# Shared PSUM slots for rarely reached entries in a graph-aggregation kernel on one Trainium2 core

## The reference

```python
mask = adj != 0
scores = where(mask, -arange(1024), -inf)
vals, idx = top_k(scores, 25);  valid = vals > -inf
feats = where(valid[..., None], x[idx], -inf)          # per batch
agg = feats.max(axis=2)
degree = mask.sum(-1)
agg = where((degree <= 25)[..., None], maximum(agg, 0.0), agg)
out = relu(concatenate([x, agg], -1) @ W + b)          # W is 256 x 128
return layernorm(x + out)                              # no affine part, eps 1e-5
```

## Time and profile before

| | |
|---|---|
| median of three runs | 766.96 us (761.51 to 767.87) |
| the profiled execution, whole | 749.41 us |
| its span, first to last instruction | 747.7 us |
| TensorE busy, mean granted clock | 585.2 us (78%), 0.922 |
| VectorE busy | 633.1 us (85%) |
| ScalarE busy | 483.4 us (65%) |
| GpSimd busy | 258.4 us (35%) |

### The profile page before, as it was taken

How to read it: one execution, slowest core, us unless ns; L and a number is a source line. 1 busy time by engine, 2 the same in 40 slices (tenths; PEclk the granted TensorE clock), 3 DMA queues, 4 the chain that set the end, 5 groups by cost and what they waited for, 6 DMA issues and landing times.

```text
span 747.7 us, 13348 instructions
## 1 busy us (share of the span) xinstructions
PE 585.2 (78%) x3952; PEld 336.8 (45%) x3952; DVE 633.1 (85%) x948; ACT 483.4 (65%) x911; POOL 258.4 (35%) x309
## 2 busy tenths in 40 slices
PE   3768878978877887888779877797887878877873
PEld 2444544644444444454444544454444444444432
DVE  5888999879987789899978788987998868988893
ACT  6735765569756687478935679465975568644654
POOL 3324413544034430455132531335403534044500
PEclk9699998999999899999988999799999989999996
DMA  7511310422024220432123120231302411011102
GB/s 248 198 36 58 116 36 19 142 61 98 1 84 141 76 76 2 133 120 77 47 79 129 57 87 31 74 133 57 111 2 75 149 56 40 2 51 33 37 1 58
DMA packets 32678, 56.68 MB, mean 76 GB/s; under 512 B 4513, under 2 KB 21154, under 8 KB 32546
## 3 DMA queue, kind: packets, MB, share of 16 engines
q1 hardware_dynamic: 26146, 42.08, 16.7%
q0 software_dynamic: 6400, 13.12, 6.3%
HBM read 50.99 MB, written 4.19 MB: 74 GB/s over the span
## 4 chain that ended last, share of the span: by engine, by line
PE 33%; DVE 23%; issue 19%; ACT 9%; DVEq 7%; another core or an unknown queue 4%; DMA 4%; SPq 1%; ACTq 0%
PE pair L946 21%; DVE part L683 9%; DVE hot L677 4%; DMA adj_sb<-in_adj 4%; PE half L946 4%; DVE agg_t L783 3%; DVEq L755 2%; PE p_V L930 2%; DVEq L815 2%; ACT maskT L480 2%; PE misc L1008 2%; DVE g_feat L754 1%; ACT row_work L611 1%; PE misc L1006 1%
## 5 line engine op out<-in xcount | busy, mean ns | idle before, releaser
L946 PE MATMUL pair<-hot,x_part 128*128 128x512 bf16 (+2 forms) x1608 | 388.3, 381 | 63.6 <-DVE part L683 36.5
L683 DVE TENSOR_REDUCE part<-pair 128x128 f32<-128x1024 f32 x256 | 311.1, 1217 | 86.7 <-PE pair L946 74.4
L946 PEld LDWEIGHTS pair<-hot,x_part 128*128 128x128 bf16 x1608 | 146.8, 101 | 228.3 <-issue 64.6
L397 POOL DMA_INDIRECT g_feat<-in_x,g_idx x200 | 191.2, 956 | 123.5 <-issue 94.8
L434 POOL TENSOR_TENSOR y_sb<-relu_sb,x_sb 128x128 f32<-128x128 f32 x64 | 30.3, 473 | 344.0 <-ACT relu_sb L539 342.8
L783 DVE TENSOR_REDUCE agg_t<-part 128x128 f32<-128x1024 f32 (+2 forms) x56 | 113.4, 2025 | 0.2 <-ACT part L546 0.2
L480 ACT ACTIVATE maskT<-p_maskT 128x1024 bf16<-128x1024 bf16 x56 | 57.0, 1018 | 54.1 <-remote 25.1
L677 DVE TENSOR_SCALAR hot<-V 128x1024 bf16<-128x1024 bf16 x224 | 84.2, 388 | 0.0
L471 ACT ACTIVATE mask<-adj_sb 128x1024 bf16<-128x1024 int32 x56 | 59.0, 1053 | 32.2 <-DMA adj_sb<-in_adj 32.0
L546 ACT ACTIVATE part<-half 128x512 f32<-128x512 f32 x56 | 33.4, 597 | 70.3 <-PE half L946 68.5
L528 ACT ACTIVATE hot<-distance,one 128x1024 bf16<-128x1024 bf16 x56 | 64.1, 1145 | 0.1
(11 more groups left out here) (86 smaller groups left out, 635.1 us busy)
## 6 DMA issues: line engine op xcount, KB each, us to landing
adj_sb<-in_adj SPq DMA_DIRECT2D x56, 512.0 KB
g_adj<-in_adj SPq DMA_DIRECT2D x8, 512.0 KB, 4.0
x_sb<-in_x SPq DMA_DIRECT2D x8, 512.0 KB
out<-y_sb SPq DMA_DIRECT2D x7, 512.0 KB
g_feat<-in_x,g_idx POOLq DMA_INDIRECT x200
out<-y_sb SPq DMA_DIRECT2D x1, 448.0 KB
w_sb<-in_W SPq DMA_DIRECT2D x1, 128.0 KB
out<-y_sb SPq DMA_DIRECT2D x1, 64.0 KB
```

Source lines behind the costliest of these rows:

```text
L397: pool.indirect_dma_start(out=g_feat[w][:, k, :], out_offset=None, in_=x_rows, in_offset=bass.IndirectOffsetOnAxis(ap=g_idx[w][:, k:k + 1] ...
L683: dve.tensor_reduce(part[:, par(q, s), BANK + p], pairs[buffer_of(s, p)][:, :, :, :].rearrange("f a k i -> f i (a k)"), AX.X, ALU.max).the ...
L946: last = pe.matmul(dst, x_part[:, q, part_no, kb], one_hot, start=(part_no == 0), stop=(part_no == 2))
```

## The change

1. `SHARED` names, for each kind of tile, three slots that several entries share. An entry is written (kb, r) with r counted from 1, and r is also the count of set columns from which a row reaches it. The members of a shared slot are picked one after the other into the same 128 columns and add up. That is right as long as no row reaches two of them.
2. `groups` replaces `banks`: slots are laid out in groups of up to eight, of nearly equal size, in the two pair buffers, a shared slot at the end of a group. Groups have 8, 8, 8, 7, 7 slots in tile 1; 8, 8, 8, 8 in tiles 2 and 3; 7, 7, 7, 7 in tiles 4 and 5; 7, 7, 6, 6 in tiles 6 and 7. A piece ends at a bank's border, at rank 6, and where a shared slot begins. The bank `half`, its copy on ScalarE and its semaphores are gone.
3. `reduce_pair` reads only the slots in use. `part` is laid out with the slices innermost, so the merge reads 4 or 5 neighbouring values for each output.
4. `count_violations` also compares the counts with `reach_tab` and marks rows that reach two members of a slot; the mark is worth `APART` = 4096 in the level. A tile so marked is picked a second time without sharing (`FULL`, 5 to 7 groups: `apart_level`, `apart_reduce`), and the extra ranks follow.
5. `p_xt` moves to the bank that `half` had (`turn`), so `rank_product` no longer waits for `s_xtc` nor `transpose_x` for the copies of V.
6. Waits on `s_half` become waits on `s_pair` and `s_xused`. `s_xused` now counts `EXTRAS` per stage.

```diff
-def banks(depths): ...
+SHARED = {1: (((0, 11), (2, 5), (3, 6), (5, 5), (6, 5), (7, 4)),
+              ((0, 10), (1, 7), (3, 5), (4, 5), (6, 4)),
+              ((0, 12), (1, 6), (2, 6), (4, 6), (5, 4), (7, 5))),
+          2: (((1, 6), (2, 4), (6, 4)),
+              ((0, 8), (2, 5), (3, 5), (4, 4), (5, 4), (7, 4)),
+              ((0, 9), (1, 5), (3, 4), (4, 5), (5, 5), (6, 5))),
+          4: (((0, 7), (1, 5), (2, 4), (4, 4), (5, 4), (6, 4), (7, 4)),
+              ((3, 4), (5, 3)),
+              ((6, 3), (7, 3))),
+          6: (((0, 7), (2, 4), (3, 4), (5, 3), (6, 4)),
+              ((0, 6), (1, 5), (4, 4), (5, 4), (7, 3)),
+              ((1, 4), (6, 3), (7, 4)))}
+SHARED.update({3: SHARED[2], 5: SHARED[4], 7: SHARED[6]})
+APART = 4096
+REDO = 2 * APART
...
+def groups(depths, shared):
+
+    taken = {member for slot in shared for member in slot}
+    own = [(kb, r) for kb, d in enumerate(depths) for r in range(d) if (kb, r + 1) not in taken]
+    slots = [[entry] for entry in own]
+    mixed = [[(kb, r - 1) for kb, r in slot] for slot in shared]
+    total = len(slots) + len(mixed)
+    count = -(-total // (2 * BANK))
...
-        part = sb("part", [P, 2, BANK + MAX_PAIRS, P], F32)
+        part = sb("part", [P, 2, P, MAX_GROUPS], F32)
...
-        half = psum("half", [P, 4, P], F32)
+        turn = psum("turn", [P, 512], F32)
...
-        p_xt = p_V[:, 0:P]
+        p_xt = turn[:, 0:P]
...
                 if not (isinstance(m, int) and m < 2):
-                    act.wait_ge(s_half, m - 1)
+                    act.wait_ge(s_xused, EXTRAS * (m - 1))
                 nc.scalar.activation(hot[:, par(q, s), 0], V[:, q, s - 1], ACT.Relu, bias=first_bias[:, 0:1],
...
-            def copy_half(i, q, s): ...
...
-                            dve.wait_ge(s_half, m - 1)
+                            dve.wait_ge(s_pair, picked_two_before(i, q, s))
...
-                dve.tensor_reduce(part[:, par(q, s), BANK + p],
-                                  pairs[buffer_of(s, p)][:, :, :, :].rearrange("f a k i -> f i (a k)"),
+                dve.tensor_reduce(part[:, par(q, s), :, p],
+                                  pairs[buffer_of(q, s, p)][:, 0:SLOTS[s][p]].rearrange("f k i -> f i k"),
                                   AX.X, ALU.max).then_inc(s_used, 1)
...
+            def apart_reduce(i, q, s):
+
+                before = EXTRAS * (pos(i, q, s) + 1) - EXTRA - len(FULL[s])
+                over = len(FULL[s]) - COUNT[s]
+                for p in range(len(FULL[s])):
+                    dve.wait_ge(s_xpair, before + p + 1)
+                    dst = part[:, par(q, s), :, p] if p < COUNT[s] else more[:, :, p - COUNT[s]]
+                    dve.tensor_reduce(dst, pairs[buffer_of(q, s, COUNT[s] + p)][:, 0:FULL_SLOTS[s][p]]
+                                      .rearrange("f k i -> f i k"), AX.X, ALU.max).then_inc(s_xused, 1)
...
-                dve.wait_ge(s_halfc, m + 1)
-                dve.tensor_reduce(agg_t[:, par(q, s)], part[:, par(q, s), 0:BANK + PAIRS[s]].rearrange("f k i -> f i k"), AX.X,
+                dve.tensor_reduce(agg_t[:, par(q, s)], part[:, par(q, s), :, 0:COUNT[s]], AX.X,
                                   ALU.max).then_inc(s_agg, 1)
...
+                for j in range(SHARES):
+                    dve.tensor_tensor(reached[:, j], cnt[:, 0], reach_tab[:, j], ALU.is_ge)
                 dve.tensor_reduce(degree[:, :], cnt[:, 0], AX.X, ALU.add)
                 dve.drain()
+                dve.tensor_reduce(sharing[:, :, :], reached[:, :, :, :], AX.X, ALU.add)
+                dve.drain()
+                dve.tensor_scalar(viol[:, 0, :, NT + 1:].rearrange("p t j -> p j t"), sharing[:, :, :], 1.5,
+                                  float(APART), ALU.is_gt, ALU.mult)
...
                     with dve.If(lv > 0):
-                        with dve.If(lv < LEVELS):
+                        with dve.If(lv < REDO):
+                            with dve.If(lv < APART):
+                                dve.sem_inc(s_xused, EXTRAS - EXTRA)
+                            with dve.Else():
+                                dve.sem_inc(s_xused, EXTRAS - EXTRA - len(FULL[s]))
+                                apart_reduce(i, q, s)
                             extra_hots(q, s)
                             extra_reduce(i, q, s)
...
-                pe.wait_ge(s_xtc, m + 1)
                 pe.matmul(p_V[:, :], rank_bf[:, :], maskT[:, par(q, s), h * N // 2:(h + 1) * N // 2],
                           start=True, stop=True).then_inc(s_Vp, 1)
...
+            def pick_pieces(q, s, pieces, dst, signal):
+                u = par(q, s)
+                for k, (kb, r, n, place, first) in enumerate(pieces):
+                    one_hot = hot[:, u, r:r + n, kb] if r < LOW else hot_high[:, u, r - LOW:r - LOW + n, kb]
+                    pick(dst[:, place:place + n], q, kb, one_hot, signal if k == len(pieces) - 1 else None,
+                         first, all(place != piece[3] for piece in pieces[k + 1:]))
```

More of the change, by code:

```diff
@@ L91, in runs @@
         return list(zip(starts, starts[1:] + [NT]))
+    ALIKE = [(a, max(t for t in SHARED if SHARED[t] == SHARED[a])) for a in SHARED
+             if a == min(t for t in SHARED if SHARED[t] == SHARED[a])]
+    REACHES = 1 + sum(len(slot) for a, _ in ALIKE for slot in SHARED[a])
     TABLES = 8 + sum(len(runs(DEPTHS[kind[0]])) for kind in KINDS)
@@ L168, in build @@
         shift = sb("shift", [P, 2, NT], F32)
-        pairs = [psum(f"pair{i}", [P, 2, 4, P], F32) for i in range(2)]
-        half = psum("half", [P, 4, P], F32)
+        pairs = [psum(f"pair{i}", [P, 2 * BANK, P], F32) for i in range(2)]
+        turn = psum("turn", [P, 512], F32)
         p_maskT = psum("p_maskT", [P, N], BF16)
@@ L771, in redo @@
                 dve.wait_ge(s_ft, m + 1)
-                dve.wait_ge(s_halfc, m + 1)
-                for p in range(BANK + PAIRS[s]):
-                    last = dve.tensor_copy(part[:, par(q, s), p], p_xt)
+                for p in range(COUNT[s]):
+                    last = dve.tensor_copy(part[:, par(q, s), :, p], p_xt)
                 last.then_inc(s_xdone, 1)
```

223 lines of the change are left out of this document (120 added, 103 removed).

## The result

| | before | after |
|---|---|---|
| median of 4 runs | 767.41 us (761.51 to 768.3) | 802.13 us (796.61 to 811.78) |
| profiled execution, span | 747.7 us | 797.2 us |
| granted clock of TensorE | 0.922 | 0.933 |

The recorded ratio is 1.0589, with a 95% interval of 1.0503 to 1.0675. Ratios in this document compare only each kernel's fast executions, within 1.5% of its fastest, while medians take all of them, so the two can differ. Here the medians are 4.5% apart, and the eight times behind them don't reproduce 1.0589, so take the loss as 4.5 to 5.9%. Forecast were 732 us and a range of 702 to 772; by either figure the time lies above it.

The account below looks back on a forecast made before the run. VectorE was taken as the pacemaker, with some 10 us a batch lost at handovers. From 749.4 us, minus 70 for shorter stages, plus 36 for second pickings, came 715, or 732 us on the median; range 702 to 772.

Parts of the forecast that it names:

- VectorE's work: Shorter picking reductions and merges, plus the sharing test, take VectorE from 77.3 to 62.7 us a batch.
- 285 more cost 0.8 us a batch: TensorE's picks: a matmul costs its columns plus 2.7 ns, so 576 a batch for 291 add 0.8 us.
- rival 3: Narrow picks on TensorE cost 83 ns, not 56: 69 us more, 801 us, slower; chance 0.07.
- 10 us per batch "lost at handovers": VectorE is the pacemaker, busy 77.3 of 87.6 us a batch; the rest is idling once a stage for one picking.
- forecast length of 78.5: Sum of the seven forecast stage lengths of a batch, 78.5 us for 87.6, so -9.1 us a batch.
- The handover that was to be late next: At stage ends TensorE waits for VectorE's last reduction and s_xused: 1.4 us idle, 2.6 us after stages 1 to 3.
- Stage 6: VectorE sets this stage, 9.9 us of work plus 0.5: 10.4 us for 12.38.
- Second pickings: Three tiles meet in a shared slot and are picked afresh: +36 us together, between 20 and 45.
- Rival 1: Larger saving: 10 us more of the waits behind xt_sb and 8 us from fewer 1.2 GHz stretches, 714 us; chance 0.17.
- Rival 2: TensorE is late more often, each new bubble bringing a 1.2 GHz stretch: 31 us come back, 763 us; chance 0.18.
- Rival 4: Far jumps over the second picking's code cost 2 us in each of 56 stages: +112 us, 844 us; chance 0.05.
- Rival 5: The change doesn't do what it says: no tile meets in a slot (695 us), or many do; chance 0.03.

Follow-up runs that it names:

- series 1: First follow-up series, parts of the change by themselves: layout of part, one-slot picks, both kernels without tile 0's gathers; the kernel before took 701.51 us.
- b_nogather2: Kernel before without the gathers of tile 0's neighbours: 695.07 us, ratio 0.939, where the kernel before took 748.93 us.
- a_nogather2: Changed kernel without tile 0's gathers, second pickings still in it: 703.26 us, ratio 0.950 to the kernel before at 748.93 us.
- series 4: Fourth follow-up series, on where late signals come from: three kernels without gathers, one with wide picks and no second pickings; the kernel before took 748.93 us.
- a_extract: Changed kernel with tile 0's extraction steps of stages 1 to 3 one reduction earlier: 780.84 us, ratio 1.035 to the kernel before.
- series 2: Second follow-up series, on second pickings and handover: changed kernel, without second pickings, with earlier extraction, and the kernel before again; the kernel before took 753.58 us.
- a_nogather: Changed kernel without tile 0's gathers, run where the kernel before took 701.51 us: 704.35 us, ratio 1.005.
- series 3: Third follow-up series, narrow picks where signals are late: changed kernel, the same with wide picks, kernel before with one-slot picks or part's layout; before took 759.72 us.
- a_wide_ns: Changed kernel with wide picks in place of the shared entries and without the three second pickings: 705.79 us, ratio 0.955 to the kernel before.
- a_nosecond: Changed kernel with a threshold of 99.5 in the sharing test, so without the three second pickings: 734.4 us, ratio 0.964 to the kernel before.
- b_narrow2: Kernel before with every picking one slot wide, 852 picking matmuls a batch for 291: 859.75 us, ratio 1.139 to the kernel before.
- b_part: Kernel before with only the layout of part changed, slices innermost: 676.6 us, ratio 0.967 to the kernel before.

## Why the prediction was wrong, step by step

**VectorE's work: right.** Merges of 512 elements at 675 ns (forecast 680), of 640 at 808 (810), reductions of 768, 896 and 1024 elements at 959, 1087 and 1225 ns (949, 1083, 1217), 546.7 us busy in all. The writes of part at a step of 20 bytes cost at most 4 to 10 ns each.

**"285 more cost 0.8 us a batch": the step that failed.** The 56 ns of the earlier trace rows are right, in series 1 for runs of 24 and in after between halts. What is wrong is the conclusion that a narrow matmul beside a weight load costs only its columns whatever the state of the signals; the sum had no term for late signals at all, though "remote" stands in the earlier trace rows. Under late signals each one more costs 21 to 25 ns, through halts and a lower clock, not through a wider spacing. An estimate for after from that price: 2280 more (6445 - 3952 weight loads, less the 213 of second pickings) x 22 ns = 50 us, 6.3 us a batch where 0.8 stood. This brought the time to where rival 3 had it (801), but rival 3 gave another mechanism, 83 ns for each pick at all times, and series 1 refutes that, and the 81 ns quoted beside it, with runs of 24 at 56 ns. That part of the agreement is luck. By the Trainium skill (TensorE: Matmul & The Clock Gate, Architectural detail) TensorE's queue takes 64 instructions; in the stretch shown, 54 lie between the signal's due time and the first halt behind 346.28, which agrees roughly. Elsewhere it doesn't: counted from the pick whose signal is late to the next halt, the same trace has anything from 3 to 75 instructions at 30 places. A full queue would explain why wide picks suffer less, since a place in it then holds up to four times as much work, but no run measured it, and why TensorE halts stays open.

**The 10 us per batch "lost at handovers": misread, the second step that failed.** The forecast took the distances between VectorE's busy time and the length of a stage in the earlier trace rows to be handovers and carried them over. The kernel without gathers shows what they were. The same batch of b_nogather2 and of a_nogather2:

```profile
sum 81.30, PE 69.28 PEld 39.96 DVE 77.09 ACT 60.80 POOL 7.82; mean PE 9.90 PEld 5.71 DVE 11.01 ACT 8.69 POOL 1.12
```

```profile
sum 76.01, PE 67.02 PEld 53.54 DVE 61.04 ACT 57.40 POOL 7.81; mean PE 9.57 PEld 7.65 DVE 8.72 ACT 8.20 POOL 1.12
```

With 77.1 us of work VectorE needs 81.3, so 4 of the 10 us were handovers and the other 6 went with the gathers. And the saving there is 81.3 - 76.0 = 5.3 us in this batch, not 9.1. Over the six batches that have neither a second picking nor the shorter end, the means are 81.4 and 76.7 us: 4.7 us a batch, over 7.7 batches 36 us. The stages with second pickings are 42 us longer in that trace, so the changed kernel should be 6 us slower without gathers; measured, it is 8.2 (series 4) and 11.8 us (series 1).

With gathers the same six batches take 88.8 us in the trace of before and 89.6 in that of after. So the gathers add 7.4 us a batch to the one and 13.0 to the other: the changed kernel's batches are 4.7 us shorter without gathers and 0.8 longer with them. (The traced execution of before is 18 us below its median; by the medians and the 43 us of second pickings they would be 1.0 shorter with them.) So most or all of the saving goes, and this comparison needs no price for a narrow pick. The forecast length of 78.5 is near the 76.7 without gathers.

**The handover that was to be late next: it isn't.** Forecast was that TensorE idles 2.6 us at the entry to stage 4 in every batch. In a_nogather2:

```profile
255.15 0.38 PE L1002 MATMUL p_V<-maskT,rank_bf 128*128 128x512 bf16 x1
255.84 1.31 PE L1018 MATMUL pair<-hot,x_part 128*128 128x512 bf16 x9 [0.31 <-DVEq L940]
```

and on VectorE at the same time:

```profile
255.35 1.23 DVE L726 TENSOR_REDUCE part<-pair 128x128 f32<-128x1024 f32 x1 [1.52 <-PE pair L1018]
256.49 1.22 DVE L784 MAX8 g_val<-g_score 128x8 f32<-128x1024 f32 x1
```

The first picks of stage 4 start at 255.84, while the last reduction of stage 3 is still under way and MAX8 has not begun. The releaser is DVEq, VectorE's sequencer, which had raised s_xused by then, ahead of its engine. I had read the code as if the count were raised behind the work. A picking's own wait is for the reduction two before it. This fits a_extract, which gained nothing. All waits in front of picks 512 wide, the first of every stage among them, come to 36.7 us in a_nogather2, 4.6 a batch; the forecast had 3 x 2.6 + 4 x 1.4 = 13.4. Its 0.5 us for branch and semaphores had no row behind it either.

**Stage 6: 10.4 forecast, 12.5 measured, 12.8 without gathers.** VectorE's work there fell from 11.91 to 10.09 us and the stage kept its length. The forecast took the larger of two bounds, VectorE's work or TensorE's with a handover. Here is VectorE in a_nogather2, from the last reduction of stage 6 to the merge that ends the window:

```profile
283.44 0.96 DVE L726 TENSOR_REDUCE part<-pair 128x128 f32<-128x768 f32 x1 [1.81 <-PE pair L1018]
...
284.56 3.42 DVE L813 TENSOR_TENSOR g_feat<-g_feat 128x1536 f32<-128x1536 f32 x3 [0.17 <-issue]
...
289.21 1.08 DVE L726 TENSOR_REDUCE part<-pair 128x128 f32<-128x896 f32 x1
```

The window begins at 277.40. TensorE needs until 283.4 for the picks, products and linear layer of stage 6, and VectorE waits for it; then come, one behind the other on VectorE, a reduction, gathered_max from 284.56 to 289.2 and the next stage's first reduction, while TensorE in turn waits 2.5 us, as in the earlier trace rows. TensorE's part and VectorE's part lie in series, 6.0 + 6.8 us, and neither got shorter: the reductions and merge that did lie beside TensorE's part.

**Second pickings: right in kind, 7 to 16 us low.** 45 to 52 us by series 2, 43 by the lengths of stages, for 36. The three stages that hold them are 15.8 (stage 3), 15.8 (stage 6) and 11.1 us (start of the first batch) longer than their like, for 14.1, 12.7 and 9.3. The extra one-hots stand behind the fresh reductions and both engines take turns in it.

**Rival 1** (a larger saving, 714): no. Its clock came, its time didn't: in the seven windows summed above TensorE has its full clock throughout in a_nogather2, where b_nogather2 has 0.86 and 0.89 in the last two. **Rival 2** (TensorE late more often, half clock, 763) named the right place, a loss in the stages TensorE sets, but it priced a lost clock, and the mean clock rose from 0.922 to 0.933. **Rival 4** (far jumps): no; at the forward jump into stage 4 shown above TensorE waited 0.31 us in all, all its picks of a_nogather2 and of a_nogather waited for issue 3.1 and 12.2 us, where 112 were priced, and VectorE's reductions waited 3.3 us for issue in the whole span of after, for 3.6 before. **Rival 5**: no; tiles meet as counted.

**The sum.** From the changed kernel's mean excess over before in series 2, 3 and the first comparison, (25.8 + 16.8 + 34.7) / 3 = 26 us, take 45 for second pickings and 50 for narrow matmuls: all else saved 69 us, against 70 forecast. That looks better than it is. The subtraction takes for granted that the parts add, and series 4 says that they don't quite: a_wide_ns, which has both costs out but for 816 narrow matmuls (18 us at 22 ns), is 43 us under before by the medians and 33 by the ratio, so all else saved 51 to 61 there. And two errors cancel in the 70: handovers priced too high in after, and distances in before that were late signals. Without gathers the same parts saved only about 36 us. Why they save more under late signals isn't settled; the move of the turned features to a bank of their own, which takes TensorE's 16.1 us of waits behind xt_sb away, is a candidate that wasn't run by itself.

**What would be better.** The kernel before with the layout of part alone beats both: 0.967 in series 1 and 0.988 [0.978, 0.998] in series 3. Sharing slots pays only if it adds few matmuls, and if no tile of the data needs a second picking: a_nosecond, without them, stands at 0.964, and with both costs out of the way a_wide_ns at 0.955; both leave out work that the result needs.

## What to carry to other kernels

Count instructions as well as columns: here a narrow matmul that cost nothing extra in one condition cost 21 to 25 ns more when TensorE's signals came late, so fewer, wider instructions are an insurance. A distance between the busiest engine's time and a stage's length is not a handover until the waits in it have been named; waits put down to "remote" on one core can be signals that came late (the copies of V above were not), and the next change can put them on the path. And run the kernel before beside each experiment: the same kernel took 701.5 and 748.9 us on one chip. And a count raised by an engine's sequencer can be ahead of that engine's last instruction: read the releaser (DVE or DVEq) before pricing the wait.

## What the runs showed of the hardware

- In all traces with gathers in series 2 to 4 and in the first comparison some of TensorE's signals came late; the longest such wait of a reduction was 4.5 us in after and 5.3 in b_narrow2. In the four traces without gathers no wait in front of VectorE's reductions or ScalarE's copies of maskT and xt_sb is put down to "remote". In series 1 they were on time in spite of the gathers. The kernel before took 701.5 us there and 748.9 to 767.4 elsewhere.
- Under late signals each 128-column matmul with its weight load that took the place of a part of a wider one cost 21 to 25 ns (100 us for 4488 more, 30 to 37 us for 1464 fewer), and otherwise 0 to 1 ns (3.7 us or 0.7 us for 4488).
- A float32 maximum by VectorE of 1024 elements for each of 128 partitions took 1905 ns when it read them at steps of 512 bytes and 1208 ns when the eight values of a maximum lay together (b_part). For 4 values lying together it took 675 ns, (675 - 203) / 456 = 1.04 ns an element, against 1.74 at the old steps.
- VectorE's sequencer raised a count while the engine's reduction before it was still under way: TensorE's picks started at 255.84 us, the reduction ran from 255.35 for 1.23 us (a_nogather2).
